# Rank counts moved from VectorE to GpSimd and TensorE, and another order of the last jobs, in a fused Mamba, attention and FFN kernel

## The reference

```python
keep_fraction = sigmoid(cond @ score_w + score_b)              # one per batch
keep = norm(x, rows) >= the (keep_fraction * 1024)-th largest norm
xm = x * keep
xn = rmsnorm(xm) * rms_w;  xi, z = split(xn @ in_proj)
xi = silu(causal_conv(xi) + conv_b)                            # 512 channels, 4 taps
dt, Bm, Cm = split(xi @ x_proj);  delta = softplus(dt @ dt_w + dt_b)
h = exp(delta * A) * h + (delta * xi) * Bm                     # scan over rows, 16 states
y = sum_states(h * Cm) + xi * D
x = x + xm + (y * silu(z)) @ out_proj
q, k, v = x @ Wq.T, x @ Wk.T, x @ Wv.T                         # 16 heads
a = einsum(cond @ Wt.T, q);  qmod = einsum(a, q)               # one query row per batch
o = softmax(where(mask, qmod @ k / 4, lowest)) @ v @ Wo.T
x = x + w3 @ gelu(h2 @ gelu(h1 @ (silu(w1 @ o) * (w2 @ o))))
```

## Time and profile before

| what | value |
|---|---|
| runs | 555.91, 560.53, 567.94 us (median 560.53) |
| the profiled execution, its own time | 556.44 us |
| its span in the profile | 554.6 us |
| PE busy | 462.9 us (83%) |
| DVE busy | 458.0 us (83%) |
| ACT busy | 381.1 us (69%) |
| POOL busy | 379.3 us (68%) |
| chain that ended last | PE 41%, DVE 30%, issue 14%, ACT 10%, POOL 3% |

### The profile page before, as it was taken

How to read it: one execution, slowest core, us unless ns; L and a number is a source line. 1 busy time by engine, 2 the same in 40 slices (tenths; PEclk the granted TensorE clock), 3 DMA queues, 4 the chain that set the end, 5 groups by cost and what they waited for, 6 DMA issues and landing times.

```text
span 554.6 us, 7884 instructions
## 1 busy us (share of the span) xinstructions
PE 462.9 (83%) x2753; PEld 332.0 (60%) x2753; DVE 458.0 (83%) x529; ACT 381.1 (69%) x664; POOL 379.3 (68%) x229
## 2 busy tenths in 40 slices
PE   8968898768858998898679998886997958899992
PEld 6423765445547665765576557554896746777651
DVE  3879799998999799779997997899999989932412
ACT  3675687679977787868877978798668778701210
POOL 5029867866999688839995897599889969500001
PEclk9987899978999999989999999899999979999897
DMA  8330111110001111110121111100111490047004
GB/s 285 124 118 38 39 38 39 38 43 38 32 28 55 40 40 38 41 38 5 36 77 39 38 40 40 40 27 32 56 40 38 189 385 7 1 156 290 1 1 157
DMA packets 17920, 38.88 MB, mean 70 GB/s; under 512 B 1666, under 2 KB 10498, under 8 KB 17875
## 3 DMA queue, kind: packets, MB, share of 16 engines
q1 hardware_dynamic: 17874, 38.32, 19.4%
HBM read 36.08 MB, written 2.23 MB: 69 GB/s over the span
## 4 chain that ended last, share of the span: by engine, by line
PE 41%; DVE 30%; issue 14%; ACT 10%; POOL 3%; DVEq 0%; POOLq 0%; ACTq 0%
DVE scanmem L1779 19%; PE hT L871 8%; DVE yTd L1790 6%; PE pp L567 5%; PE pp L660 4%; PE yacc L631 3%; PE dA L833 2%; ACT dA L1302 2%; PE pp L609 2%; POOL scanmem L1458 2%; PE yacc L627 1%; DVE yTd L1704 1%; PE pp L623 1%; ACT hc L1312 1%; PE pp L732 1%
## 5 line engine op out<-in xcount | busy, mean ns | idle before, releaser
L1458 POOL TENSOR_TENSOR scanmem<-par,scanmem 128x1024 f32<-128x1024 f32 x128 | 300.3, 2368 | 80.4 <-PE hT L871 61.0
L871 PE MATMUL hT<-con,scanmem 128*128 128x128 f32 x1024 | 161.0, 287 | 63.2 <-DVE yTd L1790 42.9
L1302 ACT ACTIVATE dA<-par,Aneg 128x512 f32<-128x512 f32 x256 | 172.0, 690 | 44.4 <-DVE scanmem L1779 42.8
L871 PEld LDWEIGHTS hT<-con,scanmem 128*128 128x128 f32 x1024 | 118.7, 146 | 119.2 <-DVE yTd L1790 39.9
L1779 DVE TENSOR_TENSOR_SCAN scanmem<-dA,carry,scanmem 128x512 f32<-128x512 f32 x128 | 156.2, 1264 | 9.7 <-ACT dA L1302 8.4
L1779 DVE TENSOR_TENSOR_SCAN scanmem<-dA,scanmem 128x512 f32<-128x512 f32 x128 | 148.8, 1204 | 10.2 <-ACT dA L1302 8.4
L1312 ACT ACTIVATE hc<-hT,CTs 128x512 f32<-128x512 f32 x128 | 86.8, 678 | 31.1 <-PE hT L871 31.0
L631 PE MATMUL yacc<-con,hc 128*128 128x128 f32 x512 | 82.1, 286 | 0.3 <-ACT hc L1312 0.3
L1790 DVE SCALAR_TENSOR_TENSOR yTd<-hT,CTs,yTd 128x512 f32<-128x512 f32 x91 | 66.1, 726 | 10.2 <-PE hT L871 10.0
L631 PEld LDWEIGHTS yacc<-con,hc 128*128 128x128 f32 x512 | 64.8, 150 | 0.6 <-ACT hc L1312 0.6
L567 PE MATMUL pp<-xnT,wi 128*128 128x512 f32 x120 | 59.1, 621 | 2.5 <-ACT xnT L1075 1.3
(11 more groups left out here) (199 smaller groups left out, 522.4 us busy)
## 6 DMA issues: line engine op xcount, KB each, us to landing
scanmem<-brow SPq DMA_DIRECT2D x32, 512.0 KB, 3.5
par<-in SPq DMA_DIRECT2D x1, 4096.0 KB, 17.4
scanmem<-in SPq DMA_DIRECT2D x1, 4096.0 KB, 14.7
xt<-in SPq DMA_DIRECT2D x4, 512.0 KB, 6.8
wi<-in SPq DMA_DIRECT2D x2, 1024.0 KB, 7.8
out<-par SPq DMA_DIRECT2D x4, 512.0 KB, 4.1
aw<-in SPq DMA_DIRECT2D x5, 256.0 KB, 6.4
xr<-in SPq DMA_DIRECT2D x1, 1024.0 KB, 9.9
```

Source lines behind the costliest of these rows:

```text
L871: last = nc.tensor.transpose(hT[:, i % 2, m * P:(m + 1) * P], hb[:, n % RING, m, i * P:(i + 1) * P], ident)
L1302: A(dA[:, m % 2, :], delta(c)[:, m, :], ACT.Exp, scale=Aneg[:, m * NS + s:m * NS + s + 1]).then_inc(da_ready, 1)
L1458: nc.gpsimd.tensor_tensor(hb[:, n % RING, ms, :], dx(c)[:, ms, :], Bb[:, row:row + 1, :].to_broadcast([P, 2, T]), ALU.mult).then_inc(bx_re ...
```

## The change

It has two parts.

Batch 1's ranks. The eight counts on VectorE go. GpSimd makes eight comparisons of 128x1024 (ones and zeros, L1600 of the new file) into buffers that are free then, ahead of its input steps 3, 5, 7 (two each), 9 and 12 (one each). Four new TensorE jobs K sum these over the rows: each is 16 products of a 128x128 block of a comparison with a column of ones. They stand in half-slots 17, 18, 20 and 23, that is in steps 8 to 11, and VectorE reads each (L1800, L1803, 128x8). `kept` of batch 1 is formed at the end of step 12 instead of step 8. The score mask moves from step 0 to step 18, and the DMA of its source row from the head of the SP queue to a place ahead of piece 11 of the B rows (chunk 1), with a new load of 512 KB (`w_outT`) behind it.

The tail. The last chunk's part of A, (x + out_proj·s)·u, is taken apart: OU makes out_proj·u once (step 30); RX turns the last chunk's rows before their update (half-slots 20 and 22 of the last chunk) and AX multiplies these by u (half-slot 26); after the last step only AP (four products of 512 columns, from the gated states `s`) and AT (turning the result) are left, and VectorE adds. The order O0, O1, R0, R1, A, G, GT, M, RR becomes O0, AP, O1, AT, G, R0, GT, M, R1, RR. The fillers ahead of both R, A, G and M go (12 products), AT gets 4, S1's go from 12 to 10. O waits for one gated piece at a time. The softmax takes its maxima in the instruction that adds the mask (L1621 and L1624 become a product with a reduction), the exp is made in two halves, and PT starts behind the first. The output of batch 0 (FB) is written out in parts of 2, 2 and 4 row tiles, with five output DMAs instead of four.

```diff
+COUNT_AT = [17, 18, 20, 23]
+COMPARE_AT = {3: (0, 1), 5: (2, 3), 7: (4, 5), 9: (6,), 12: (7,)}
+RANKED_AT, MASK_AT = 12, NS + 2
...
+    tail += [("Y", last, 1), ("Y", last, 3), ("O", last, 0), ("AP", 1, 0), ("O", last, 1), ("AT", 1, 0), ("G", 1, 1), ("R", last, 0), ("GT", 1, 0),
+             ("M", 1, 0), ("R", last, 1)]
+    tail += attention_jobs(1)[6:]
...
+            def job_K(job, o):
+
+                j = job[2]
+                pe.wait_ge(compared, 2 * (j + 1))
+                for g in range(GB):
+                    for i in range(2):
+                        last = mm(o[:, g:g + 1], above[2 * j + i][:, g * P:(g + 1) * P], ones[:, :], start=i == 0, stop=i == 1)
...
+            def job_AP(job, o):
+
+                e = NCH - 1
+                pe.wait_ge(gated, 2 * (e + 1))
+                for i in (1, 3):
+                    wait_read(pe, ("Y", e, i))
+                for m in range(CT):
+                    last = mm(o[m * QR:(m + 1) * QR, :], wou[:, m, :], dx(e)[:, m, :], start=True, stop=True, tile_position=(0, m * QR))
...
+                g = GB + i
+                nc.gpsimd.tensor_scalar(above[i], magrow, ss[:, g:g + 1], 1.0, ALU.is_lt, ALU.mult).then_inc(compared, 1)
...
-                return V.tensor_tensor(sm[:, 0:512], o, negm[:, 0:512], ALU.add)
+                return V.tensor_tensor_reduce(out=sm[:, 0:512], in0=o, in1=negm[:, 0:512], scale=1.0, scalar=-FLT_MAX, op0=ALU.add, op1=ALU.max, accum_out=st[:, 4:5])
...
-                own.mark(V.reduce_max(st[:, 0:1], sm[:, 512:1024], AX.X))
+                V.tensor_scalar(st[:, 1:2], st[:, 0:1], -1.0, None, ALU.mult).then_inc(mx_ready, 1)
+                dve.wait_ge(p_ready, 2 * (b + 1))
...
-                    if c == 0:
-                        batch1_rows(s)
+                    if n == RANKED_AT:
+                        batch1_rows()
+                    if n == MASK_AT:
+                        score_mask()
```

More of the change, by code:

```diff
@@ L112, in all_slots @@
             beside[3] += [("U", 0, 0)]
+            for j, h in enumerate(COUNT_AT):
+                beside[h] += [("K", 0, j)]
         else:
@@ L120, in all_slots @@
         beside[2 * (NCH - 1) * NS + ATT[i]] += [job]
+    beside[2 * NS + OU_AT] += [("OU", 1, 0)]
+    for j, h in enumerate(RX_AT):
+        beside[2 * (NCH - 1) * NS + h] += [("RX", 1, j)]
+    beside[2 * (NCH - 1) * NS + AX_AT] += [("AX", 1, 0)]
     for i, job in enumerate(attention_jobs(1)[:2]):
@@ L124, in all_slots @@
     tail = []
-    for s, jobs in sorted(epilogue_slots(NCH - 1).items()):
-        tail += jobs
-    tail += attention_jobs(1)[2:]
+    last = NCH - 1
+    tail += [("Y", last, 1), ("Y", last, 3), ("O", last, 0), ("AP", 1, 0), ("O", last, 1), ("AT", 1, 0), ("G", 1, 1), ("R", last, 0), ("GT", 1, 0),
+             ("M", 1, 0), ("R", last, 1)]
+    tail += attention_jobs(1)[6:]
     tail += [("W12", 0, 0), ("WT", 0, 0)]
@@ L307, in build @@
         junk = yTd[:, 1, :, :].rearrange("p a b -> p (a b)")
+        above = [par[1][:, a, i * S:(i + 1) * S] for a in (3, 2) for i in range(2)] + [junk, x1T[:, 1, :], negm[:, :], par[1][:, 3, 0:S]]
         mrow = x1T[:, 1, 0:S // 4].bitcast(U8)
@@ L473, in _ @@
                         sp.wait_ge(bx_ready, 2 * BROWS * (piece - BSLOTS + 1))
+                    if piece == PIECES + BSLOTS:
+                        sp.wait_ge(ranked, 3)
+                        sp.dma_start(mrow, mask[0:1, :].to_broadcast([P, S])).then_inc(s_mrow, 16)
+                        sp.dma_start(woutT, w_outT.rearrange("(k p) o -> p k o", p=P)).then_inc(s_wout, 16)
                     slot = piece % BSLOTS
@@ L730, in scores @@
                 wait_read(pe, ("RR", job[1], 0))
+                if (job[1], j) == (1, 1):
+                    for i in range(2):
+                        wait_read(pe, ("R", NCH - 1, i))
                 for k in range(KD):
@@ L1182, in ev_R, with ev_OU, ev_AP, ev_RX @@
                 return A(dst, o.rearrange("p (k i t) -> p k i t", k=KD, i=2), ACT.Copy)
+            def ev_OU(job, o):
+                return A(wou[:, :, 0:NH], o[:, 0:CT * NH].rearrange("p (m h) -> p m h", m=CT), ACT.Copy, scale=0.5)
+            def ev_AP(job, o):
+                wait_read(act, ("PT", 0, 0))
+                return A(apart, o, ACT.Copy)
+            def ev_RX(job, o):
+                return ev_R(("R", NCH - 1, job[2]), o)
             def ev_A(job, o):
@@ L1198, in softmax @@
                 act.wait_ge(mx_ready, b + 1)
-                A(sm[:, :], sm[:, :], ACT.Exp, bias=st[:, 1:2], accum_out=st[:, 2:3]).then_inc(p_ready, 1)
+                for h, total in ((0, 2), (1, 5)):
+                    half = sm[:, h * 512:(h + 1) * 512]
+                    A(half, half, ACT.Exp, bias=st[:, 1:2], accum_out=st[:, total:total + 1]).then_inc(p_ready, 1)
             def ev_PT(job, o):
@@ L1687, in read @@
                         last.then_inc(freed(job), 1)
-                if job[0] == "S0":
-                    wait_read(dve, job)
-                    own.mark(V.reduce_max(st[:, 4:5], sm[:, 0:512], AX.X))
                 if job[0] == "S1":
@@ L1749, in _, with score_mask, batch1_rows @@
                 read(("D", 0, m))
[L1751 to L1764 removed]
+            def score_mask():
+                dve.wait_ge(s_mrow, 16)
+                V.tensor_scalar(negm[:, :], mrow, -1.0, FLT_MAX, ALU.add, ALU.mult)
+            def batch1_rows():
+                dve.wait_ge(rstd_ready, 2)
+                wait_read(dve, ("K", 0, GB // 2 - 1))
+                kept(slice(GB, 2 * GB), 1)
             def scan_step(n, m):
```

142 lines of the change are left out of this document (93 added, 49 removed).

## The result

The changed kernel took 586.98, 587.75, 589.24 and 592.58 us (median 588.5); the kernel before, beside it, 555.91, 560.53, 567.94 and 568.72. The last two of these are executions in a slower state that shows in some runs of the same kernel at a lower granted clock, so the ratio, 1.0554 with an interval from 1.0435 to 1.0672, goes by the other two, in the mean 558.2: slower by 24 to 38 us, far outside the range that was given. The profiled execution took 586.98 us with a span of 585.2, 30.6 more than before's 554.6.

What follows compares the result with a forecast made beforehand. VectorE bounds steps 4 to 8, nothing is full in 9 to 12, PE is the tail's chain. Terms -4.7 + 3.5 + 2.65 + 0.3 + 0.7 - 1.3 - 3.75 = -2.6: 553.8 against 556.44, plus 1.0: 555 us; range 546 to 564.

Steps and rivals of the forecast that it cites:

- Counts away: Steps 5 to 8: four of the eight counts leaving VectorE tell, -4.7 us; bounds -9.5 and 0.
- Comparisons on GpSimd: GpSimd, mainly 79 to 117 us: eight comparisons at 1.04 us each, 8.3 against 7.6 idle, cost 0, up to about +2.
- the ring: GpSimd's inputs, made ahead into a ring of four: the cover by which the comparisons were taken to cost 0.
- Rival (e): Steps 4 to 9: comparisons delay GpSimd's inputs, scans wait for those, the 4.7 us are lost, 558.5 us; chance 0.05.
- K on TensorE: Steps 8 to 11: four K of 3.2 us, 13.0 in all, partly hidden, cost +3.5 us; bounds 0 and +8.0.
- PE that is busier may hold the clock: TensorE, 117 to 140 us: with K beside other work a higher granted clock could win back up to 4.1 us.
- `kept`: End of step 12: batch 1's keep mask waits for GpSimd as at step 8, +2.65 us; bounds 0.55 and 3.2.
- Mask 0, SP 0, OU +0.3: Score mask at step 18: 0, up to +2.4; SP loads ahead of piece 11: 0, up to +2; OU job: +0.3 us.
- Softmax of batch 0: Last chunk: 0.69 and 0.97 us of VectorE go, second exp and added sum cost 0.35: -1.3; bounds -1.7 and +0.5.
- RX/AX: Jobs in scan steps of the last chunk, PE work about that of A, half hidden: +0.7 us; bounds with OU 0 and +3.
- Tail: After the last step: shorter chain on PE from O to scores, softmax and output, -3.75 us; bounds -6 and +1.
- rival (d): Tail: with 12 fillers gone PE's clock falls, 6 us of PE work become 12, 559.8 us; chance 0.05.

Runs made afterwards that it cites:

- cmp_mul: Changed kernel with products in place of GpSimd's comparisons (ranks wrong), K jobs kept; scans of step 13 start 18.08 us later than before, whole time not given.
- no_k_mul: cmp_mul without the K jobs and their reads, a copy of the norms standing in; scans of step 13 start 2.42 us later than before, whole time not given.
- a_wide: Changed kernel, its comparisons as they are, with each K product moving 64 columns of ones instead of one; 574.66 and 575.40 us, ratio 1.032.
- k_wide: cmp_mul with each K product moving 64 columns of the identity instead of one column of ones (ranks left out); 558.64 us in one execution.
- a_alone: Kernel before with only the change of the rank counts (comparisons, K jobs, later masks), old tail; 587.17 and 592.23 us, ratio 1.0602.
- b_fix: Kernel before with only the change of tail and last chunk, but batch 0's exp in one instruction again; median 553.72 us, ratio 0.996.
- b_fix_k9: b_fix with batch 1's keep mask moved from step 8 to the end of step 9; median 556.49 us, ratio 0.9982.

## Why the prediction was wrong, by its steps

**Counts away, -4.7: right.** With comparisons of 1.12 us steps 8 and 9 were 5.2 to 5.5 early (`cmp_mul`, `no_k_mul`), and as forecast step 9 gained nothing more from the mask's leaving. By step 12 of `no_k_mul` 3.3 of it were left.

**Comparisons on GpSimd, 0 (up to +2): wrong, the largest miss.** The step priced them by the earlier trace rows, a product, and called this the nearest row. The shape was the same; the operation was not, and no row of before had it. 3.70 instead of 1.04 us is 29.6 instead of 8.3, and the cost was 18.4 us by step 12. Bounding from one row on one side made the range too narrow. A second fault made it worse: the step spoke of the inputs that the ring covers and did not list what else stands in GpSimd's queue, the ends of two convolutions and the sums, for which X and VectorE wait. Rival (e) had the engine, at +4.7 and 0.05, but another wait: scans for their inputs, not X for the convolutions.

The page that it cited (the Trainium skill, Perfetto Trace Analysis, "Optimizing Scalar/DVE Operations") speaks against such a move because the two engines share a port. The outcome is as it warns, the reason is not: VectorE's scans took 2.33 us a pair beside the comparisons, as before; it was GpSimd's own time, and the place in its queue.

**K on TensorE, +3.5 (0 to +8): wrong.** K cost 13.1 us by step 12 alone and 9.9 on top of the comparisons, and 3.2 more in the wait for Z. The passes were priced right (3.2 forecast, 3.6 measured at the high clock), and with 64 columns K would have cost less than forecast: 0.4 us (`a_wide`) to 1.8 (`k_wide`) by step 12 and up to 0.95 for Z. What failed is "PE that is busier may hold the clock", for products of one column: TensorE was busy for 23.00 of 23 us at 0.51, K took 6.8 us, and the transposes and D behind it twice their time. For products of 64 columns it came true, 1.00 from 113 to 126 where it is 0.50 without K. The row that priced K stood between products of 128 and of 16 columns, at the high clock, and could not show this.

**`kept`, +2.65 (0.55 to 3.2): right.** In the changed kernel its three instructions take the time from 173.85 to 176.49, 2.64 us, the first two waiting for GpSimd as at step 8 and the third not. That it came to the hundredth is luck, since in `cmp_mul` the same three take 4.87, end of step 12, timeline of VectorE:

```profile
158.60 1.43 DVE L1831 TENSOR_SCALAR keep<-cnt,fr 128x8 f32<-128x8 f32 x1
160.06 1.19 DVE L1833 TENSOR_SCALAR keep<-keep 128x8 f32<-128x8 f32 x1
161.16 2.38 DVE L1834 TENSOR_TENSOR scl<-keep,lnv 128x8 f32<-128x8 f32 x1
```

Here all three wait one after the other, each for the next end of a GpSimd instruction; the third for a product of 2.33 us (161.18 to 163.51 in GpSimd's timeline). By the rule that the prediction weighed and left out (the Trainium skill, SBUF — State Buffer, "Who interferes with whom"), a VectorE instruction with two SBUF inputs waits for a GpSimd instruction that reads SBUF, if that one comes first. That the third can wait agrees. Which came first the rows don't tell: in `cmp_mul` the third's record starts 0.02 us before GpSimd's product and it waited, after the change 0.01 before one (176.41 and 176.42) and it did not.

**Mask 0, SP 0, OU +0.3: right.** From step 13 to 51 nothing moves: the mask at step 18, the loads and OU cost less than 0.05 us together, on this path.

**Softmax of batch 0, -1.3, and RX/AX, +0.7: wrong in sign, +4.3 together** (from +30.31 at step 57 to +34.63 at step 63). "The second exp's own start and the added sum cost some 0.35" failed: the sum of the two halves, 128x1, has two SBUF inputs and waited 3.40 us for GpSimd (L1749, timeline of VectorE after):

```profile
480.29 3.40 DVE L1749 TENSOR_TENSOR st<-st 128x1 f32<-128x1 f32 x1 [1.59 <-ACT sm L1291]
```

It ends where GpSimd's second product from there does, at 483.7. The instruction that it replaced, the joining of two maxima, is the same kind. In `a_alone`, with before's softmax and other phases, that one took 4.70 us, and there too the last chunk lost 3.6; its timeline of VectorE:

```profile
480.33 4.70 DVE L1665 TENSOR_TENSOR st<-st 128x1 f32<-128x1 f32 x1
```

So what such a small instruction costs is not its own: 0.16 us in the tail, where GpSimd is idle, 0.97, 3.40 or 4.70 by what GpSimd has under way. Between steps 58 and 60, where the second RX stands, `b_fix` loses another 2.1 (from -2.64 to -0.57); that it is RX's doing was not shown by itself.

**Tail, -3.75: about right**, -3.1. By its parts, on TensorE after (O L685, AP L703, G L758, scores L807):

```profile
525.67 3.72 PE L685 MATMUL pp<-wo,par 128*128 128x256 f32 x16 [0.51 <-DVE par L1669]
529.32 1.06 PE L703 MATMUL pp<-par,wou 128*32 128x512 f32 x8
...
535.79 0.64 PE L758 MATMUL pp<-xt,a_sb 128*32 128x256 f32 x8
...
541.25 4.88 PE L807 MATMUL pp<-x1T,r_sb 128*128 128x512 f32 x8
```

From the first O to G 10.1 us instead of the 12.0 of the earlier trace rows, to the scores 15.6 instead of 17.1: 1.5 of the 2.7 that were forecast. O did not start earlier against the last gate (-1.2 forecast). AP's four products took 1.06 us, not 1.8: each writes its own quarter of the rows of the output, and in the rows its eight passes of 0.6 us overlap. The other 1.6 us of the tail's gain lie behind the start of the scores and were not taken apart. The scores took 4.88 instead of 3.67, at a granted clock of 0.73 instead of 1.00, as rival (d) had it, but this did not decide.

Comparisons and K are 31.5 us (18.4, 9.9 and 3.2) where 3.5 were forecast. `k_wide`, with short comparisons and a K near its price, shows what would have come: 558.64 us in one execution, against the forecast 555.

## What to carry to other kernels

Price a moved instruction by a row of the same operation on the same engine; a row of the same shape with another operation is no bound, and where there is none, say that the upper end is open and measure it alone first. When an in-order engine takes on work, list everything behind it in its queue, and who waits for each. For jobs put beside other work on TensorE, look at the granted clock, and try them with more columns even if the result doesn't need them. Keep tiny VectorE instructions out of stretches in which GpSimd is busy, if a row shows that such an instruction waits there. And when an experiment puts a stand-in for what it drops, look what the stand-in costs.

## What the runs showed of the hardware that was not expected

- GpSimd's `is_lt` of 128x1024 takes 3.63 us with a constant and 3.70 with a column, a product of the same shape 1.12: 3.3 times.
- A TensorE that is busy for all of 23 us, 9.5 of them with products of one column, was granted 0.51; with 64 columns in the same products 0.93, and without the jobs 0.80. The second job took 3.7 instead of 6.8 us: the wider products were the faster ones.
- A VectorE instruction of 128x1 with two inputs (a sum, a maximum) took between 0.16 and 4.70 us, and three of 128x8 in a row, two of them with one tensor input, between 0.5 (`b_fix_k9`) and 4.87.
